# Sixteen query projections against twenty-four layernorm tiles: the same work in another order

## What is computed

```python
x = x + attn(layernorm(x), wq, wk, wv, wo)     # 16 heads of 128, causal, 4 x 2048 x 2048
x = x + ffn(layernorm(x), w_gate, w_up, w_down)  # hidden size 8192, silu(gate) * up
def _layernorm(x, axis=-1, eps=1e-5):
    m = jnp.mean(x, axis=axis, keepdims=True)
    v = jnp.var(x, axis=axis, keepdims=True)
    return (x - m) / jnp.sqrt(v + eps)
```

## Time and profile before

| | |
|---|---|
| runs of the kernel | 2897.06, 2901.34, 2959.34 us; median 2901.34 |
| the profiled execution, its own time | 2891.49 us |
| its span (first to last instruction) on core 6, the slowest | 2889.3 us |
| spans of the other cores | 2868.9 to 2888.0 us |
| TensorE busy over the span | 2431.8 us, 84% |
| VectorE, ScalarE busy | 557.6 us, 551.1 us, 19% each |
| mean granted TensorE clock, cores 0 to 7 | 0.946 to 0.951 |

### The profile page before, as it was taken

How to read it: one execution, slowest core, us unless ns; L and a number is a source line. 1 busy time by engine, 2 the same in 40 slices (tenths; PEclk the granted TensorE clock), 3 DMA queues, 4 the chain that set the end, 5 groups by cost and what they waited for, 6 DMA issues and landing times.

```text
span 2889.3 us, 31752 instructions; the slowest of 8 cores (2868.9 to 2889.3 us)
## 1 busy us (share of the span) xinstructions
PE 2431.8 (84%) x12111; PEld 1143.1 (40%) x12352; DVE 557.6 (19%) x978; ACT 551.1 (19%) x1090; POOL 169.8 (6%) x324
## 2 busy tenths in 40 slices
PE   2666888888888888749779999999999999797886
PEld 1333344444444444414334444444444444343333
DVE  4322233333333333304300001000100000000000
ACT  4433233333323333302210000000000000000000
POOL 0000000000000000010000000000000011111110
PEclk9888999999999999959889999999999999898988
DMA  5433210101010101073244444545444545655554
GB/s 179 109 103 80 44 23 16 22 16 22 16 22 16 22 16 23 1 145 117 79 87 76 77 77 75 79 75 79 74 79 74 79 65 75 115 76 110 92 96 90
DMA packets 61491, 196.36 MB, mean 68 GB/s; under 512 B 6944, under 2 KB 6944, under 8 KB 56096
## 3 DMA queue, kind: packets, MB, share of 16 engines
q0 software_dynamic: 46080, 134.24, 30.1%
q1 hardware_dynamic: 15264, 60.07, 6.3%
HBM read 311.72 MB, written 16.78 MB: 114 GB/s over the span
## 4 chain that ended last, share of the span: by engine, by line
PE 79%; ACT 7%; DMA 5%; issue 5%; DVE 4%; SPq 0%; DVEq 0%; ACTq 0%; POOL 0%; POOLq 0%
PE psA L719 8%; PE psB L730 8%; PE psA L395 4%; PE psF L730 4%; PE psD L719 4%; PE psA L415 4%; PE psA L804 4%; PE psB L395 4%; PE psB L804 4%; PE psB L415 4%; PE psE L730 4%; PE psC L719 4%; PE psA L332 2%; PE psB L332 2%; DMA x2r<-x2s 2%
## 5 line engine op out<-in xcount | busy, mean ns | idle before, releaser
L719 PE MATMUL psA<-h_fm,wg 128*128 128x512 bf16 x1004 | 226.6, 381 | 10.4 <-issue 9.4
L730 PE MATMUL psB<-h_fm,wu 128*128 128x512 bf16 x1004 | 225.0, 379 | 1.1
L461 ACT ACTIVATE p_sb<-psA,stats 128x1024 bf16<-128x1024 f32 x96 | 103.6, 1079 | 545.9 <-PE psA L445 284.7
L719 PE MATMUL psD<-h_fm,wg 128*128 128x512 bf16 x512 | 194.0, 379 | 1.1
L730 PE MATMUL psF<-h_fm,wu 128*128 128x512 bf16 x512 | 194.0, 379 | 1.1
L719 PE MATMUL psC<-h_fm,wg 128*128 128x512 bf16 x491 | 186.1, 379 | 0.0
L730 PE MATMUL psE<-h_fm,wu 128*128 128x512 bf16 x491 | 186.1, 379 | 0.0
L804 PE MATMUL psB<-wd,hidden 128*128 128x512 bf16 x502 | 153.4, 385 | 19.4 <-DVE osb L818 18.8
L804 PE MATMUL psA<-wd,hidden 128*128 128x512 bf16 x501 | 152.8, 384 | 6.1 <-DVE osb L818 3.8
L528 DVE CAST pt<-psD 128x512 bf16<-128x512 f32 x192 | 115.7, 602 | 209.7 <-PE psD L515 209.7
L719 PEld LDWEIGHTS psA<-h_fm,wg 128*128 128x128 bf16 x1024 | 100.2, 98 | 131.6 <-issue 11.8
(11 more groups left out here) (124 smaller groups left out, 2987.7 us busy)
## 6 DMA issues: line engine op xcount, KB each, us to landing
wg<-wg_t POOLq DMA_DIRECT2D x64, 512.0 KB, 5.9
wu<-wu_t POOLq DMA_DIRECT2D x64, 512.0 KB, 5.9
wd<-wd_t POOLq DMA_DIRECT2D x128, 256.0 KB, 4.1
xt<-xkv SPq DMA_DIRECT2D x16, 1024.0 KB, 4.8
wqbuf<-wq_t POOLq DMA_DIRECT2D x16, 512.0 KB, 5.0
xt<-xq SPq DMA_DIRECT2D x8, 1024.0 KB, 9.4
wkbuf<-wk_t POOLq DMA_DIRECT2D x16, 512.0 KB, 5.1
wvbuf<-wv_t POOLq DMA_DIRECT2D x16, 512.0 KB, 5.0
```

The lines of the kernel that those rows point to most:

```text
L461: t_exp = P.do("scalar", lambda e, s=s, slo=slo, shi=shi, sec=sec, sc_t=sc_t, sstat=sstat: e.activation(sb["p_sb"][:, P_OFF[s] + slo:P_OFF ...
L719: t_gmm = P.do("tensor", lambda e, hc=hc, c=c, half=half, par=par, gb=gb: e.matmul(bk(gb[half]), wg[par][:, c, :], sb["h2_fm"][:, c, half ...
L730: t_umm = P.do("tensor", lambda e, hc=hc, c=c, half=half, par=par, ub=ub: e.matmul(bk(ub[half]), wu[par][:, c, :], sb["h2_fm"][:, c, half ...
```

## The change

The order of tiles and query heads is changed. A helper `emit_ln_tile` holds what both loops did for a tile; a counter gives it the buffers in turn. Now eight pairs come first, a tile of `xq` and a tile of `xkv`, with no head between them. Then follow eight rounds with one of the remaining tiles of `xkv` (8 to 15) and two query heads each. `emit_q_head` itself, its single weight buffer and all sizes stay.

```diff
-    for qt in range(NQ):
-        par = qt % 4
...
+    _tcnt = [0]
+
+    def emit_ln_tile(src_dr, row0, dst_fn):
+        par = _tcnt[0] % 4
+        _tcnt[0] += 1
+        t_ld = P.dma("sync", lambda e, row0=row0, par=par: e.dma_start(
+            out=xt[par][:, :], in_=src_dr[row0:row0 + 128, :]),
             [xt_free[par]], "ld")
...
+    for t in range(8):
+        emit_ln_tile(dr["xq"], t * 128,
+                     lambda c0, qt=t: sb["h1q"][:, c0:c0 + 4, qt * 128:(qt + 1) * 128])
+        emit_ln_tile(dr["xkv"], t * 128,
+                     lambda c0, i=t: sb["h1_fm"][:, c0:c0 + 4, i * 128:(i + 1) * 128])
...
-    for i in range(NKT):
...
-        emit_q_head(i)
+    for i in range(8, NKT):
+        emit_ln_tile(dr["xkv"], i * 128,
+                     lambda c0, i=i: sb["h1_fm"][:, c0:c0 + 4, i * 128:(i + 1) * 128])
+        emit_q_head(2 * (i - 8))
+        emit_q_head(2 * (i - 8) + 1)
```

More of the change, by code:

```diff
@@ L302, in emit_program @@
     htm_free = [None] * 4
-    for qt in range(NQ):
-        par = qt % 4
-        t_ld = P.dma("sync", lambda e, qt=qt, par=par: e.dma_start(
-            out=xt[par][:, :], in_=dr["xq"][qt * 128:(qt + 1) * 128, :]),
+    _tcnt = [0]
[4 more added lines that the diff above has]
+            out=xt[par][:, :], in_=src_dr[row0:row0 + 128, :]),
             [xt_free[par]], "ld")
@@ L311, in emit_program @@
         htm_free[par] = emit_transposes(
-            htm[par], NKT,
-            lambda c0, qt=qt: sb["h1q"][:, c0:c0 + 4, qt * 128:(qt + 1) * 128],
-            lambda c: [t_norm[c // 4]])
+            htm[par], NKT, dst_fn, lambda c: [t_norm[c // 4]])
+    for t in range(8):
[3 more added lines that the diff above has]
+                     lambda c0, i=t: sb["h1_fm"][:, c0:c0 + 4, i * 128:(i + 1) * 128])
     t_h1q_done = P.tok("act")
```

## The result

The changed kernel is slower: its time stands to that of the kernel before as 1.023 to 1, with a 95% interval of 1.021 to 1.0251. The medians of ten runs each are 2969.59 and 2930.85 us, only 38.7 us apart; they hold runs in which one die ran at a lower clock, and the ratio leaves those out. The profiled execution took 2967.05 us, its span is 2964.8 us on core 6, 75.5 us more than the 2889.3 before.

A forecast was written before the change was run, and what follows sets the result against it. Chains of waits, not an engine's rate, were taken to bound the part before 317.96 us. 59.6 - 53.2 + 50.4 + 9.0 = +65.8 us gave 2957, or 2966 us on the median's scale, 2.3% more; range 2941 to 2988.

The forecast's parts named there:

- item 4: Odd heads: the clock falls to half in the pause, so they take 9.4 us, even heads keep 8.28; +9.0 us.
- the upper bound of 6.4 us for the pause: Between a round's two heads: 0.55 us to the issue plus 5.86 to the third head's start is enough.
- item 3: Between a round's two heads: the single buffer's weight load is wholly exposed, 8 x 6.3 = +50.4 us.
- the zero for all that lies behind the heads: Everything after the last head runs the same lists and only shifts with it, adding nothing.
- Eight tiles ahead: Before the first head: eight tiles done without a head, 8 x 7.45 = +59.6 us, nothing added for their loads.
- Turns: From one round's heads to the next: eight turns fewer, 8 x 6.65 = -53.2 us; seven stay.
- The last step, from the profiled execution to the median of the runs: Whole kernel: the median, 2901.3 us, lies 10 us above the profiled execution, so 2957 becomes 2966 us.
- Less dear: Rival, pause between heads: the clock stays up (+47) or the pause is 5.5 us (+55); +40 to +58 us, chance 0.33.
- Dearer: Rival, pause between heads: pause of 7.9 us and odd heads of 10.3 us, sum +86 us; chance 0.07.
- Not slower: Rival, heads back to back: full clock and saved turns pay for everything, only with a pause under 1.6 us; chance 0.02.
- Given back later: Rival, stages behind the heads: a different clock gains 8 us there, bringing the change within 2%; chance 0.04.

The follow-up runs named there:

- two-buffer run: The changed kernel with a second weight buffer, used by the odd heads: ratio 1.0024 to the kernel before.
- busy pause: The changed kernel with 30 matmuls that nobody needs between the two heads of a round: ratio 1.0167 to the kernel before.
- with halves: The changed kernel with its one weight buffer loaded in two halves, the first issued before the head's end: ratio 1.0113 to the kernel before.
- statistics ahead, two buffers and the old order: The kernel before with two weight buffers and the next tile's statistics and normalised pieces written ahead of the head: ratio 0.9696 to the kernel before.
- statistics ahead and one buffer: The kernel before with its one weight buffer, the next tile's statistics and normalised pieces written ahead of the head: ratio 1.0024 to the kernel before.
- statistics ahead and two buffers, in the new order: The changed kernel's order with two weight buffers and the next tile's statistics and pieces ahead of the heads: ratio 0.9832 to the kernel before.

## Where the prediction held, and the step that failed

The forecast was +65.8 us, 2.3%. The ratio of the runs gives 2.3%, and the last head of core 6 ends 66.7 us later. The mechanism was right: what was moved, the bare load and the falling clock are all in the trace.

The step that failed is the size of item 4, the clock, on the core that the sum was made for: +9.0 us forecast, +3.6 measured. Even heads did not keep their 8.28 us there. Two smaller steps failed with it: the upper bound of 6.4 us for the pause in item 3, and the zero for all that lies behind the heads. By its items, on core 6:

1. Eight tiles ahead: forecast +59.6, measured +60.5 (first head at 146.27 instead of 85.76). Tiles kept their pace and the loads stayed hidden.

2. Turns: forecast -53.2. In the changed kernel 238.37 - 136.00 - 54.8 = 47.6 us are seven turns of 6.8 us, so -52.2.

3. The pause for weights: forecast 8 x 6.3 = +50.4, measured +54.8, 6.9 us each on this core. The upper bound of 6.4, taken from the third head's start, failed here: it held for transfers that land in 5 us, and in this execution core 6 had 6. The two-buffer run shows that the pause was the cause: without it 1.023 became 1.002.

4. The clock: forecast +9.0, measured 136.00 - 132.43 = +3.6. Odd heads took 9.1 us, not 9.4, and even heads 7.9 instead of the 8.28 that were to stay. That the falling clock makes odd heads slow, the busy pause showed by itself. Why even heads were shorter on this core wasn't looked for.

The errors of items 3 and 4 are 4 to 5 us each and cancel on core 6. That is luck only in part: pause and odd head together take 15.5 to 16.0 us on every core, so a longer pause is followed by a shorter head. In the mean over the eight cores no item is off by more than 0.3 us: +59.9 for the tiles, -52.9 for the turns, +50.3 for the pauses (6.3 us each) and +8.8 for the heads (odd 9.4, even 8.3), together +66.1 us.

Behind the heads the forecast had zero. The span of core 6 grew by 75.5 us, 8.8 more than its heads. Its first matmul of the down projection starts 67.0 us later than before, so the rest arises behind it, in code that is the same. On core 3 nothing arises there: its down projection starts 71.3 us later and its span is 72.1 us longer. In the mean of the cores 3.7 us arise behind the heads. No experiment looked at it, and its cause stays open; the ratio of 1.023, taken over runs, is 67 us of 2900.

The last step, from the profiled execution to the median of the runs, did not hold either. It took 2901.3 us, the median of three runs, for the kernel before. The median of ten is 2930.85, and by the medians as they stand the change is 38.7 us, 1.3%, just under the low end of +40.

Rivals. "Less dear" rested on a clock that stays up through the pause, or on a short pause. The clock fell. What a clock that stays up would have been worth the busy pause measured: 18 us. Pauses were short on cores 0, 3, 5 and 7, 5.7 to 6.0 us, but the odd heads there took 9.7 to 9.9 us and not 8.8. "Dearer" is out with 6.9 us at most as a core's mean. "Not slower" needed a pause under 1.6 us; with halves it was still about 3. With no pause at all, in the two-buffer run, the last head of the four cores without 0.81 ended at 313.6 us in the mean. That is 5.5 us before the 319.1 of the kernel before and not 12.8, since even heads still took 8.2 to 8.3 us. "Given back later" is out: no stage behind the heads got shorter by the 8 us that it needed, and attention took 1.3 us more on core 6.

By the fit of the Trainium skill, page "DMA: Bandwidth & Descriptors", section "Anatomy of one DMA — SWDGE (gpsimd) path", a transfer of 1 MiB was estimated at 4.4 us, the pause at 4.95 and the sum at +55. Measured are landings of 5.0 to 6.1 us as medians of the cores and pauses of 5.7 to 6.9, so for the transfer the fit was too low by 0.6 to 1.7 us here.

## What to carry to other kernels

A single buffer is free as long as something else of the same length stands beside its transfer. Before work is moved, ask of each buffer what covers its load now, and what will after. Two waits of the same length side by side must be removed together: each alone gave nothing here (0.9997 and 1.0024), both gave 3%.

The time of a gap on TensorE isn't only its own length, since much of what follows a gap of 4 to 7 us ran at half clock here. A head took 7.07 us with no such gap before it, 8.3 with transposes between the gap and the head, and 9.0 to 9.4 with the gap directly before it. So a gap cost 1.2 us on top of its length in the one place and 1.9 to 2.4 us in the other.

## What the runs showed of the hardware that was not expected

The same 512 KB load from GpSimd lands mostly in about 5.0 or about 6.0 us, and which one depends on the core and the execution: medians 5.0 and 6.0 on cores 5 and 6 of one execution, 5.0 on core 6 of another. It can be slower still: with statistics ahead, two buffers and the old order the medians of the cores are 7.0 to 8.0 us, in a stretch where the DMA engines were busy 0.61 of the time instead of 0.28. No wait came of it there. The cause wasn't looked for.

A granted clock of 0.81 over whole heads appeared on pairs of cores: 0, 1, 4 and 5 of the changed kernel with two buffers, 2 and 3 with the busy pause. A head then takes 8.58 us instead of 7.07. It doesn't need heads that stand back to back: in the old order it held in pieces for 97 us on cores 2 and 3 with two buffers, and for 99 us on cores 0 and 1 with statistics ahead and one buffer. The Trainium skill, page "TensorE: Matmul & The Clock Gate", section "Part 1: The HAM clock gate (the "warmup" mystery)", tells of a current limiter that takes a die to 13/16 of the clock once three of its cores run dense matmuls. The value agrees, 13/16 being 0.81, but here it stood on two cores of a die with the others at 1.00 or at their two levels. And the densest heads had none of it: with statistics ahead and two buffers, in the new order (pairs back to back, turns of 2.03 us) as in the old, the stretch of the heads reads 1.00 on every core. What sets it off stays open.
